# Four layers of conditioning and routed experts on 2048 tokens: routing matmuls reordered, expert places filled before the last shared down, a third job ahead of the experts, the last half as one program

## The chip, the cores and the metric

The kernel runs on one core of one Trainium2 chip. What is told is the device time of one execution in microseconds (us). The core has five engines that run their own instruction streams and wait for each other by semaphores: TensorE (PE, matmuls), VectorE (DVE), ScalarE (ACT), GpSimd (POOL) and SyncE (SP, which here only starts transfers); sixteen DMA engines move the data.

## The reference, cut to what matters

x is 2 x 1024 x 256 in float32. Four layers follow each other, each with a half that brings in the condition and a network half. The changed places lie in these halves:

```
swiglu(h) = (silu(h @ gate) * (h @ up)) @ down                             # 256 -> 512 -> 256
L0 ffn:  i = argmax(h @ gate_w)  (32 experts)
         x + swiglu_shared(h) + swiglu_i(h * sigmoid(max(h @ gate_w)))
L2 cond: s = sigmoid([h, t_emb] @ W_router.T); top 2 of 8 by s + bias, gates s / sum(s)
         (mean of 2 shared swiglu + sum of gates * gelu(h @ r_w1.T) @ r_w2.T) / 4
L2 ffn:  top 2 of 8 by softmax(h @ gate_W.T)
         x + 0.5 * shared swiglu (8 of width 128, mean) + 0.5 * gated swiglu of width 1024
L3 cond: as L2 cond, with one shared swiglu, divided by 3
L3 ffn:  top1 of 16 by softmax(h @ Wg); each expert takes its 160 tokens of highest probability
         y = h, and for taken tokens y = gelu(h @ W1 + b1) @ W2 + b2;   x + y
```

The output is x after the last layer, in float32.

## The kernel before, in words

A half is one `nc.Block`: a program for each engine, with a barrier at its end. In `half_l0`, `half_cond` (called for layers 2 and 3) and `half_ffn2` it runs in this order: the router's logits and their transposition (`pe_logits`, `pe_turn`); the first pieces of the shared unit; the places of the tokens among the experts' rows; the rest of the shared jobs; the routed experts; the jobs that are left, and the mixes.

The shared unit is class `Glu`. A job is 512 tokens through one unit. It has four up parts (`up_part`), each of which makes 128 columns of gate and up product in two banks of three pairs, and one `down`. Every matmul is split into three (`matmul_split`, L319 to L321) over high and low parts of both operands: `weights_high`, `features_high`, `hidden_high` are casts on ScalarE (L467, L459, L480), `weights_low`, `features_low`, `hidden_low` subtractions on VectorE (L491, L485, L504). Between up and down stand `silu` (L473, ScalarE) and `multiply` (L498, VectorE); a part of the same pair of banks waits for the multiply three parts earlier. `pe_jobs`, `act_jobs` and `dve_jobs` write out the order; `beside` is called behind each multiply, `between` behind each job. The number `split` says how many jobs precede the experts: four of eight in layer 2's cond half and in its network half, two of four in layer 3's cond half and in layer 0.

The places are class `Slots`: `scan` (L1252) on VectorE, `pe_places` (L1259 to L1265) on TensorE, `places` (L1272 to L1288) on VectorE, which gives each token its row, four times `mark` (L1297 to L1310) beside the parts, `pe_trace` (L1317, 32 or 16 groups of small matmuls) and `rows_of` (L1324 to L1331), from which gathers and scatters take their indices. In the cond halves the scatters L1458 write the rows sorted by expert to memory; they are paced by the multiplies, four for each step, and the experts load them from there (L586).

`LaneExperts` (layer 0) runs 24 rounds: in each, four lanes' weights are copied from the load's buffer `big` to their places in `space` (L1068), two parts on ScalarE and VectorE each, and then multiplied (L1106). `SplitGluExperts` (layer 2's network half) runs 39 tiles; its weights are cast to a high half by ScalarE (`own_highs`, L930) and a low one by VectorE (`own_lows`, L935). Both wait at their start for all shared downs, since the places lie in the shared unit's memory. In the trace, the last adds of the shared jobs are L1477 (layer 0), L1745 (layer 2's network half), L1608 and L1609 (cond halves); L1090, L943 and L661 turn the first rows of the experts. The mixes of the cond halves are L1717 and L1720, two adds for each of a chunk's four token tiles.

The last half is three programs. A route block (L3014) writes the rows to `by_token` and makes marks, trace and rows. `stage_sorted_biased` gathers row tiles (POOL L2785, two tiles for each semaphore), turns them (L2811), runs up (L2823), bias, gelu, turn (L2833) and down (L2844) for 31 tiles, adds the second bias (L2906) and scatters the results (L2795); the experts' weights come through a ring of four (`wring`, L2776, 1.4 MB each). Beside the tiles VectorE searches for each expert the bit pattern of the 160th highest probability, one bit in a tile (`try_bit`, L2914 to L2922), and TensorE sums the tally (L2851). `stage_kept_and_stored` ranks equal values, makes `keep` and `drop` (L2968 to L2983), adds both kinds of tokens (L2985, L2991; 16 each) and stores.

## Time and profile before

| what | us |
|---|---|
| median of three runs | 1734.08 |
| lowest and highest | 1731.73, 1737.95 |
| profiled execution | 1737.56 |
| its span in the trace | 1735.8 |

| stretch of the profiled execution (us from the start of the span) | what runs |
|---|---|
| 30.7 to 275 | layer 0, network half (lane rounds 93 to 262) |
| 409 to 689 | layer 2, cond half |
| 690 to 1276 | layer 2, network half (tiles 786 to 1190) |
| 1279.5 to 1511 | layer 3, cond half (experts 1365 to 1460) |
| 1511 to 1540 | route block of the last half |
| 1540 to 1711.7 | 31 tiles |
| 1711.8 to 1735.8 | kept and stored |

In the whole span TensorE is busy 1482 us (85%), VectorE 991 (57%), ScalarE 657 (38%), GpSimd 426 (25%), and the mean granted clock of TensorE is 0.915 of full speed. A share of the span says little here, since every stage has its own limit. The rows below are to be read by the idle time in brackets: it stands in front of the instruction, with what ended it.

### The profile page before, as it was taken

What the parts mean: (1) busy time and instruction counts of PE and PEld (TensorE: products, weight loads), DVE (VectorE), ACT (ScalarE), POOL (GpSimd) and SP (SyncE); (2) the same over time, 40 slices, a digit from 0 to 9 for tenths busy, and PEclk for the clock granted to TensorE, in tenths of its full rate; (3) what the DMA queues carried; (4) which work ended last, traced back from release to release, by engine and by line L of the source; (5) the groups of instructions that cost most, each with busy time, mean ns of one, the idle gap of its engine ahead of it and who ended that gap; (6) DMA issues with size and microseconds to landing.
All of it is one profiled execution on the core that took longest, in us unless ns stands there. A gap on an engine that the chain in (4) does not pass through costs nothing. (4 is left out here: it accounts for less than half of the span.)

```text
span 1735.8 us, 25954 instructions
## 1 busy us (share of the span) xinstructions
PE 1482.4 (85%) x8354; PEld 1126.5 (65%) x8354; DVE 991.0 (57%) x1782; ACT 657.1 (38%) x977; POOL 426.1 (25%) x366
## 2 busy tenths in 40 slices
PE   8787888765989997897999999999967799749992
PEld 5632334633877786786888888887856677526661
DVE  5566675435644364645877776774645334447675
ACT  3175775212233332224655555553322233201110
POOL 1512221000434400010343343331007243023420
PEclk9899999967899999898999999999987899859996
DMA  5268972352223240230222202204022233245823
GB/s 188 87 255 314 343 251 93 120 170 98 92 92 101 80 143 28 76 152 4 95 101 87 111 28 101 98 19 146 1 97 85 91 109 130 67 163 186 269 90 112
DMA packets 82918, 211.38 MB, mean 122 GB/s; under 512 B 10785, under 2 KB 57762, under 8 KB 74594
## 3 DMA queue, kind: packets, MB, share of 16 engines
q1 hardware_dynamic: 66944, 166.40, 26.9%
q0 software_dynamic: 15840, 43.27, 7.4%
q8 instruction: 76, 1.25, 0.3%
q14 instruction: 56, 0.46, 0.1%
q10 hardware_dynamic: 2, 0.00, 0.0%
HBM read 165.21 MB, written 44.43 MB: 121 GB/s over the span
## 5 line engine op out<-in xcount | busy, mean ns | idle before, releaser
L630 POOL DMA_INDIRECT results<-sb_big,sb_s_out_row x63 | 132.4, 2101 | 466.4 <-ACT sb_big L861 304.5
L935 DVE TENSOR_TENSOR sb_h_split<-sb_big,sb_h_split 128x2048 fp32r<-128x2048 f32 x78 | 178.5, 2289 | 87.9 <-ACT sb_h_split L930 87.9
L930 ACT CAST sb_h_split<-sb_big 128x2048 fp32r x78 | 146.7, 1903 | 42.0 <-issue 40.5
L826 PE MATMUL ps<-sb_big,sb_e_hT 128*128 x624 | 141.0, 379 | 1.1 <-DVE sb_e_hT L979 1.1
L319 PE MATMUL ps<-sb_h_split 128*128 128x512 f32 x312 | 133.5, 428 | 9.6 <-DVE sb_h_split L954 6.9
L1068 DVE COPY sb_g_space<-sb_big 128x1024 f32 x168 | 108.4, 699 | 49.8 <-issue 22.8
L1068 ACT COPY sb_g_space<-sb_big 128x1024 f32 x120 | 118.5, 1048 | 41.6 <-DMA sb_big<-in_l_routed 21.2
L826 PEld LDWEIGHTS ps<-sb_big,sb_e_hT 128*128 128x128 f32 x624 | 118.2, 190 | 18.5 <-issue 1.3
L319 PE MATMUL ps<-sb_g_split,sb_g_ws 128*128 128x512 f32 x256 | 108.5, 424 | 23.4 <-DVE sb_g_product L498 15.7
L1458 POOL DMA_INDIRECT sorted_in<-sb_big,sb_p_slots x64 | 70.4, 1099 | 220.3 <-DVE sb_p_slots L1284 177.3
L321 PE MATMUL ps<-sb_h_split 128*128 128x512 f32 x312 | 124.1, 398 | 0.0
L320 PE MATMUL ps<-sb_h_split 128*128 128x512 f32 x312 | 123.9, 397 | 0.0
L1106 PE MATMUL ps<-sb_g_space,sb_e_rT 128*32 128x512 f32 x768 | 95.7, 616 | 21.2 <-ACT sb_g_space L1068 9.6
L592 POOL DMA_INDIRECT results<-sb_big,sb_p_out_row x78 | 77.3, 992 | 147.3 <-DVE sb_big L741 146.7
L320 PE MATMUL ps<-sb_g_split,sb_g_ws 128*128 128x512 f32 x256 | 106.4, 416 | 0.0
L321 PE MATMUL ps<-sb_g_split,sb_g_ws 128*128 128x512 f32 x256 | 105.6, 412 | 0.0
L619 POOL DMA_INDIRECT sb_big<-by_token,sb_s_in_row x63 | 63.0, 1001 | 154.0 <-DVE sb_s_out_row L1331 135.4
L319 PE MATMUL ps<-sb_g_ws,sb_g_split 128*128 128x256 f32 x256 | 78.5, 307 | 25.2 <-DVE sb_g_split L504 14.5
L473 ACT ACTIVATE sb_g_sg<-ps 128x512 f32<-128x512 f32 x64 | 38.1, 597 | 148.4 <-PE ps L321 116.6
L673 PE MATMUL ps<-sb_big,sb_x_rT 128*128 x312 | 89.1, 409 | 4.1 <-ACT sb_x_rT L718 4.0
L498 DVE TENSOR_TENSOR sb_g_product<-sb_g_sg,ps 128x512 f32<-128x512 f32 x64 | 43.8, 685 | 68.0 <-ACT sb_g_sg L473 54.2
L693 PE MATMUL ps<-sb_big,sb_x_hT 128*128 x312 | 82.4, 388 | 0.0
(450 smaller groups left out, 3210.2 us busy)
## 6 DMA issues: line engine op xcount, KB each, us to landing
sb_big<-in_l_routed SPq DMA_DIRECT2D x32, 1024.0 KB
sb_big<-in_l2f_routed SPq DMA_DIRECT2D x8, 3072.0 KB, 10.5
sb_e_wring<-in_l_experts SPq DMA_DIRECT2D x16, 1408.0 KB
sb_big<-in_l_routed SPq DMA_DIRECT2D x32, 512.0 KB
sb_big<-results SPq DMA_DIRECT2D x32, 512.0 KB, 7.2
sb_big<-sorted_in SPq DMA_DIRECT2D x18, 512.0 KB
by_token<-sb_big SPq DMA_DIRECT2D x12, 512.0 KB, 3.2
sorted_in<-sb_l1p_zero SPq DMA_DIRECT2D x2, 2048.0 KB, 9.6
```

Source lines behind the costliest of these rows:

```text
L319: pe.matmul(to, w[0], x[0], start=start, stop=False)
L320: pe.matmul(to, w[0], x[1], start=False, stop=False)
L321: return pe.matmul(to, w[1], x[0], start=False, stop=stop)
L592: pool.indirect_dma_start(out=results, out_offset=bass.IndirectOffsetOnAxis(ap=places.out_row[:, j:j + 1], axis=0), in_=self.tile(j), in_o ...
L630: pool.indirect_dma_start(out=results, out_offset=bass.IndirectOffsetOnAxis(ap=places.out_row[:, j:j + 1], axis=0), in_=self.tile(j), in_o ...
L673: last = pe.matmul(psum[:, j % 2, 0:self.NF * P], self.rT[:, j % 2, k * P:(k + 1) * P], self.w[:, e, k * self.NF * P:(k + 1) * self.NF * P ...
L693: last = pe.matmul(psum[:, 2 + j % 2, 0:D], self.hT[:, j % 2, f * P:(f + 1) * P], self.w[:, e, lo:lo + D].rearrange("p s n -> p (s n)"), s ...
L826: last = pe.matmul(psum[:, 7, 0:D], self.hT[:, f // TPC, f % TPC * P:(f % TPC + 1) * P], self.weight(place, 2 * KD * self.F + f * D, D), s ...
L930: act.copy(self.own[part][:, 0, :], self.raw(e, part)).then_inc(self.own_high[part], 1)
L935: dve.tensor_tensor(self.own[part][:, 1, :], self.raw(e, part), self.own[part][:, 0, :], ALU.subtract).then_inc(self.own_low[part], 1)
L1068: last = copy(self.own[part][:, g, :], here.rearrange("p s n -> p (s n)"))
L1106: last = pe.matmul(psum[g * W:(g + 1) * W, 2 * part + u % 2, :], self.rT[:, r % 2, k, g * W:(g + 1) * W], self.own[part][:, g, lo:lo + FU] ...
```

## The change

1. In `half_l0`, `half_cond` and `half_ffn2` ScalarE makes four weight casts instead of two ahead of the quads; TensorE runs two up parts instead of three ahead of `pe_places`, and the third and fourth behind it; VectorE puts `multiply` ahead of `features_low`, and the last two weight subtractions go from ahead of the first multiply to behind the second and third. `pe_trace` waits for the marks by quarters.
2. `LaneExperts` and `SplitGluExperts` get `act_open` and `dve_open`, which fill the first expert's places during the last shared down, each part behind its own wait (`wait_space`); VectorE's part runs ahead of the last shared add (`closing`).
3. In layer 3's cond half `split` goes from two to three, the chunk order changes, and three mixes stand at the end instead of two.
4. The last half is one block, `half_ffn3`: the writes of the rows and the loads of the first experts stand on SyncE's queue at its start, each row tile has a semaphore, gathers follow the rows directly, the search starts at 2^-7 and has 26 steps instead of 30, the ranks, the choice and the adds of the dropped stand beside the last tiles, and loads and stores follow in the same block.

```diff
-TOP_BIT = 29
+TOP_BIT = 25
+FLOOR = 2.0 ** -7
...
             def dve_jobs(self, dve, n0, n1, between=None, beside=None, closing=None):
                 for m in range(self.NF * n0, self.NF * n1):
                     n, f = divmod(m, self.NF)
+                    self.multiply(dve, m)
                     if f == 0 and n + 1 < len(self.jobs) and n + 1 != self.resume:
                         self.features_low(dve, n + 1)
-                    self.multiply(dve, m)
...
                 self.hidden_low(dve, self.NF * n1 - 1)
+                if closing is not None:
+                    closing()
                 self.add(dve, n1 - 1)
...
+            def act_open(self, act, wait_space):        # SplitGluExperts
+                for part in range(2):
+                    wait_space(act, part)
+                    self.own_highs(act, 0, part)
...
+            def dve_open(self, dve):
+                for part in range(2):
+                    self.own_lows(dve, 0, part)
...
+            def dve_open(self, dve, wait_space):        # LaneExperts
                 experts = self.experts_of(dve, 0, (0, 1, 2))
-                self.fill_dve(dve, 0, 0, experts)
-                self.fill_dve(dve, 0, 1, experts)
+                for part in range(2):
+                    wait_space(dve, part)
+                    self.fill_dve(dve, 0, part, experts)
+                return experts
...
             def pe_trace(self, pe):
                 self.wait_known(pe)
-                pe.wait_ge(self.marked, 8)
                 for n in range(self.G):
+                    if n % (self.G // 4) == 0:
+                        pe.wait_ge(self.marked, 2 * (4 * n // self.G + 1))
...
+                def wait_space(eng, part):                                   # half_l0
+                    eng.wait_ge((glu.both, glu.downed)[part], (glu.NF * split, 2 * (split - 1))[part])
...
-                        for m in range(3):
+                        for m in range(2):
                             glu.up_part(pe, m)
                         places.pe_places(pe)
-                        glu.up_part(pe, 3)
+                        for m in range(2, 4):
+                            glu.up_part(pe, m)
...
-                        for q in range(2):
+                        for q in range(4):
                             glu.weights_high(act, 0, q)
                         route.act_quads(act)
-                        for q in range(2, 6):
+                        for q in range(4, 6):
                             glu.weights_high(act, 0, q)
...
-                        for q in range(4, 6):
-                            glu.weights_low(dve, 0, q)
                         def trace(m):
+                            if m in (1, 2):
+                                glu.weights_low(dve, 0, m + 3)
...
-                chunk_order = tuple(range(NCH)) if two else (2, 3, 0, 1)
+                early = () if two else tuple(range(split))
+                chunk_order = tuple(range(NCH)) if two else tuple(range(split, NCH)) + early
...
-                        if not two:
-                            mix(0, 2)
-                            mix(1, 3)
+                        for c in early:
+                            mix(c, N - split + c)
...
+                    def _(sp):                                               # half_ffn3
+                        for c in range(NCH):
+                            sp.dma_start(chunk_of(by_token, c), ctok[:, c * TPC:(c + 1) * TPC, :]).then_inc(written, 16)
                         for e in range(RING):
                             if e >= 2:
                                 sp.wait_ge(w_in[e % 2], 8 * (e - e % 2) + e % 2)
                             sp.dma_start(wring[:, e, :], a["l3_experts"][e]).then_inc(w_in[e % 2], 16)
+                        places.wait_known(sp)
...
+                        sp.wait_ge(stored, 16 * tiles)
+                        for c in range(NCH):
+                            load_results(sp, [y], c, got[c])
...
+                            if j == TOP_BIT + 1:
+                                rank_even()
+                            if j == TOP_BIT + 3:
+                                choose_kept()
                             if j >= 1:
                                 add_b2(j - 1)
+                            if j > TOP_BIT + 3:
+                                add_dropped((j - TOP_BIT - 4) * 6, (j - TOP_BIT - 3) * 6)
                         add_b2(tiles - 1)
+                        add_dropped((tiles - TOP_BIT - 4) * 6, NT)
...
-            half_cond(3, wr3c, bias3, ("g3",), [(0, c) for c in range(NCH)], 2, a["l3c_routed"], 1.0 / 3.0, None)
+            half_cond(3, wr3c, bias3, ("g3",), [(0, c) for c in range(NCH)], 3, a["l3c_routed"], 1.0 / 3.0, None)
+            half_ffn3()
```

VectorE in layer 3's cond half, from the last step of the places to the first mark, before (`sb_g_ws` is a weight part, `sb_g_split` the features, `sb_g_product` a multiply's output):

```order
2126 L1288 TENSOR_SCALAR sb_p_tile_expert<-ps 1x39
2127 L491 TENSOR_TENSOR sb_g_ws<-sb_wbuf,sb_g_ws 128x512 x2
2128 L485 TENSOR_TENSOR sb_g_split<-sb_big,sb_g_split 128x1024
2129 L498 TENSOR_TENSOR sb_g_product<-sb_g_sg,ps 128x512
2130 L1297 CAST sb_p_tall<-sb_p_slot 128x32
```

The same place now, up to the first of the two weight subtractions:

```order
2134 L1308 TENSOR_SCALAR sb_p_tile_expert<-ps 1x39
2135 L499 TENSOR_TENSOR sb_g_product<-sb_g_sg,ps 128x512
2136 L486 TENSOR_TENSOR sb_g_split<-sb_big,sb_g_split 128x1024
2137 L1317 CAST sb_p_tall<-sb_p_slot 128x32
2138 L1318 TENSOR_SCALAR sb_p_tall<-sb_p_tall 128x32
2139 L1319 CAST sb_p_high<-sb_p_tall 128x32
2140 L1320 SCALAR_TENSOR_TENSOR sb_p_slot<-sb_p_high,sb_p_slot 128x32
2141 L1325 TENSOR_TENSOR sb_big<-sb_lanes_iota,sb_p_high 128x312
2142 L1327 TENSOR_TENSOR sb_big<-sb_big,sb_ids 128x312
2143 L1330 TENSOR_TENSOR sb_big<-sb_lanes_iota,sb_p_slot 128x1024
2144 L499 TENSOR_TENSOR sb_g_product<-sb_g_sg,ps 128x512
2146 L492 TENSOR_TENSOR sb_g_ws<-sb_wbuf,sb_g_ws 128x512
```

The multiply moved ahead of three VectorE instructions, and the weight subtractions behind the first mark.

SyncE's transfers of the last half, before: the write of the rows in a block of its own, then the ring, and at the end loads and stores behind another block's end.

```order
262 L3015 UNCONDITIONAL_BRANCH
263 L3018 DMA by_token<-sb_big 128x4x256 x4
264 L3014 UNCONDITIONAL_BRANCH
265 L2771 UNCONDITIONAL_BRANCH
266 L2776 DMA sb_e_wring<-in_l_experts 128x2816 x4
...
303 L2770 UNCONDITIONAL_BRANCH
304 L2996 UNCONDITIONAL_BRANCH
305 L1464 DMA sb_big<-results 128x4x256 x4
306 L3002 DMA out_x<-sb_big 128x4x256 x4
```

The same transfers now:

```order
262 L2811 UNCONDITIONAL_BRANCH
263 L2814 DMA by_token<-sb_big 128x4x256 x4
264 L2818 DMA sb_e_wring<-in_l_experts 128x2816 x4
...
301 L1485 DMA sb_big<-results 128x4x256 x4
302 L2829 DMA out_x<-sb_big 128x4x256 x4
```

The ring's loads stand directly behind the rows' writes, and the ends of two blocks are gone from between.

VectorE at the end of the last tiles now (L2974 adds the second bias to a tile's rows, L2969 casts the last hidden tile, L3015 adds dropped tokens, L3052 kept ones):

```order
2802 L2974 TENSOR_TENSOR sb_big<-ps,sb_e_wring 128x256
2803 L3015 SCALAR_TENSOR_TENSOR sb_big<-sb_big,sb_e_drop 128x256 x6
2804 L2969 COPY sb_e_hT<-ps 128x512
2808 L2974 TENSOR_TENSOR sb_big<-ps,sb_e_wring 128x256
2809 L3015 SCALAR_TENSOR_TENSOR sb_big<-sb_big,sb_e_drop 128x256 x6
2813 L2974 TENSOR_TENSOR sb_big<-ps,sb_e_wring 128x256
2814 L3015 SCALAR_TENSOR_TENSOR sb_big<-sb_big,sb_e_drop 128x256 x4
2815 L3052 SCALAR_TENSOR_TENSOR sb_big<-sb_big,sb_e_keep 128x256 x16
```

Before, no add of dropped tokens stood among the tiles; all sixteen stood together in the block behind them.

## Rows read from the trace of the kernel before

**Rows 1.** Busy time by stretch: window, us, busy time (and count) by engine, clock, DMA.

```profile
93.00:262.00 169.00, 137.38 (x1414) 53.63 (x1418) 115.83 (x185) 123.86 (x167) 37.51 (x35) 0.96 0.81 299
785.00:1190.00 405.00, 394.18 (x1936) 334.99 (x1937) 288.90 (x280) 225.12 (x239) 135.05 (x69) 0.98 0.19 70
1556.00:1700.00 144.00, 133.05 (x568) 87.24 (x569) 99.85 (x296) 26.92 (x61) 46.96 (x48) 1.00 0.53 179
1713.00:1719.00 6.00, 2.67 (x6) 1.67 (x6) 3.77 (x11) 0.00 (x0) 0.00 (x0) 0.50 0.97 324
```

**Rows 2.** Order of time, VectorE, layer 3 cond: start, us, instruction, idle before.

```profile
1285.77 1.29 DVE L491 TENSOR_TENSOR sb_g_ws<-sb_wbuf,sb_g_ws 128x512 fp32r<-128x512 f32 x2 [2.74 <-ACT sb_g_ws L467]
...
1298.49 0.17 DVE L1272 TENSOR_SCALAR sb_p_count<-ps 128x8 int32<-128x8 f32 x1 [6.32 <-PE ps L1259]
...
1301.85 1.27 DVE L491 TENSOR_TENSOR sb_g_ws<-sb_wbuf,sb_g_ws 128x512 fp32r<-128x512 f32 x2
...
1304.18 0.67 DVE L498 TENSOR_TENSOR sb_g_product<-sb_g_sg,ps 128x512 f32<-128x512 f32 x1
```

**Rows 3.** Order of time, TensorE, the same stretch: first, 13th and 37th matmul, next part.

```profile
1287.12 0.80 PE L319 MATMUL ps<-sb_g_split,sb_g_ws 128*128 128x512 f32 x1 [1.18 <-DVE sb_g_ws L491]
...
1292.41 0.63 PE L319 MATMUL ps<-sb_g_split,sb_g_ws 128*128 128x512 f32 x1
...
1297.94 0.39 PE L321 MATMUL ps<-sb_g_split,sb_g_ws 128*128 128x512 f32 x1
...
1304.90 0.80 PE L319 MATMUL ps<-sb_g_split,sb_g_ws 128*128 128x512 f32 x1 [4.88 <-DVE sb_g_product L498]
```

**Rows 4.** Order of time, the same waits in layer 0 and in layer 2's halves.

```profile
52.21 0.80 PE L319 MATMUL ps<-sb_g_split,sb_g_ws 128*128 128x512 f32 x1 [5.92 <-DVE sb_g_product L498]
...
429.37 0.17 DVE L1272 TENSOR_SCALAR sb_p_count<-ps 128x8 int32<-128x8 f32 x1 [5.19 <-PE ps L1259]
...
704.90 0.17 DVE L1272 TENSOR_SCALAR sb_s_count<-ps 128x8 int32<-128x8 f32 x1 [3.23 <-PE ps L1259]
```

**Rows 5.** Order of time, TensorE, the first lane round of layer 0.

```profile
94.83 1.07 PE L1106 MATMUL ps<-sb_g_space,sb_e_rT 128*32 128x512 f32 x4 [2.96 <-DVE sb_g_space L1068]
```

**Rows 6.** Order of time, start of layer 2's 39 tiles: ScalarE, VectorE, TensorE.

```profile
785.40 3.70 ACT L930 CAST sb_h_split<-sb_big 128x2048 fp32r x2 [12.20 <-issue]
...
787.52 4.49 DVE L935 TENSOR_TENSOR sb_h_split<-sb_big,sb_h_split 128x2048 fp32r<-128x2048 f32 x2 [2.46 <-ACT sb_h_split L930]
...
792.41 0.80 PE L319 MATMUL ps<-sb_h_split 128*128 128x512 f32 x1 [6.85 <-DVE sb_h_split L954]
```

**Rows 7.** Order of time, layer 3 cond, between shared jobs and experts: TensorE, GpSimd.

```profile
1331.73 0.39 PE L319 MATMUL ps<-sb_g_ws,sb_g_split 128*128 128x256 f32 x1
...
1348.49 0.97 POOL L1458 DMA_INDIRECT sorted_in<-sb_big,sb_p_slots  x1 [0.30 <-issue]
...
1351.28 0.37 PE L319 MATMUL ps<-sb_g_ws,sb_g_split 128*128 128x256 f32 x1 [1.02 <-issue]
1352.68 0.37 PE L320 MATMUL ps<-sb_g_ws,sb_g_split 128*128 128x256 f32 x1 [1.03 <-issue]
...
1365.40 0.44 PE L661 MATMUL ps<-sb_ident,sb_big 128*128 128x128 f32 x2 [0.79 <-DVE sb_big L1608]
```

**Rows 8.** Order of time, end of layer 3's cond half: last down, last two mixes.

```profile
1492.17 0.58 PE L319 MATMUL ps<-sb_g_ws,sb_g_split 128*128 128x256 f32 x1 [4.26 <-DVE sb_g_split L504]
...
1501.27 6.79 DVE L1720 SCALAR_TENSOR_TENSOR sb_big<-sb_big,sb_t_gates 128x256 f32<-128x256 f32 x16
```

**Rows 9.** Order of time, start of the last half: trace, first gather, first turn.

```profile
1532.39 7.00 PE L1317 MATMUL ps<-sb_s_marks,sb_big 128*128 128x31 f32 x32 [7.44 <-DVE sb_big L1310]
...
1540.88 0.99 POOL L2785 DMA_INDIRECT sb_big<-by_token,sb_s_in_row  x1 [78.86 <-POOLq L3014]
...
1549.50 0.69 PE L2811 MATMUL ps<-sb_ident,sb_big 128*128 128x128 f32 x2 [10.10 <-DMA sb_big<-by_token,sb_s_in_row]
```

**Rows 10.** Order of time, VectorE, kept and stored: first step, adds of the kept.

```profile
1711.82 0.43 DVE L2968 TENSOR_TENSOR sb_k_over<-sb_val,sb_cut 128x256 f32<-128x256 f32 x1 [8.25 <-PEq L2770]
...
1724.53 6.42 DVE L2991 SCALAR_TENSOR_TENSOR sb_big<-sb_big,sb_k_keep 128x256 f32<-128x256 f32 x16
```

261 lines of the change are left out of this document (120 added, 141 removed).

## Prediction

> **What bounds the kernel now.** I read first the busy time by stretch [rows 1]. In the routed rounds of layer 2's network half TensorE is busy 394 of 405 us at a granted clock of 0.98, and in the last 31 tiles 133 of 144 us at 1.00: these stretches move only if TensorE gets less to do. In layer 0's lane rounds the DMA share is 0.81, so the loads share the bound with the copies on ScalarE and VectorE. What the change can shorten lies between such stretches. So I then read, stage by stage, the rows in order of time with what ended each idle time. The reader is to see in each of them one engine waiting for a chain of small steps on another.
>
> **Routing among the first pieces, four times.** In the layer 3 cond half TensorE runs three up parts from 1287.12 and only then the matmuls for the places; VectorE has been idle 6.32 us when it gets their result at 1298.49 [rows 2, 3]. Its chain for the places runs to 1301.85; then two weight casts and a feature cast (2.33 together) and the first multiply (0.67) follow, and TensorE, which needs that multiply to free a bank, has been idle 4.88 us at 1304.90 [rows 2, 3]. After the change TensorE runs two parts before the places. It starts them 1.18 us earlier, since VectorE no longer waits 2.74 us for ScalarE's third and fourth weight cast [rows 2]: these now stand ahead of the quads, where ScalarE was waiting for the logits. Twelve matmuls make a part; the first 13 come some 0.43 us apart (12 steps from 1287.12 to 1292.41), the others 0.23 (24 steps to 1297.94), so 13 x 0.43 + 11 x 0.23 = 8.1 us and the places come at 1294.0, VectorE's chain at 1294.4 instead of 1298.5. The multiply now stands ahead of the casts, and parts 2 and 3 fill TensorE's 4.88. From there VectorE's work beside the parts is the same in sum (the two weight casts only move behind multiplies 1 and 2) and fills its time, so what the chain gains is what is gained: **4.0** here (one part, 12 x 0.23 = 2.8, and 1.18), **3.8** in layer 2's cond half (idle 5.19) [rows 4]. In layer 2's network half the idle is 3.23, and only the part's 2.8 leaves: **2.7**. Layer 0 has less work for the marks (96 columns instead of 312), so TensorE is the bound after the places, and of its idle 5.92 all but the wait of about 1 us for the later quads is filled: **4.9** [rows 4]. The lows are bounded by 0 (the freed time is taken by the marks, which TensorE's trace then awaits in quarters), the highs by TensorE's own idle, 4.9 to 5.9.
>
> **First experts' places filled early.** In layer 0 TensorE waits 2.96 us for the first filled place at 94.83 [rows 5]; ScalarE's two and VectorE's two fills now run beside the last shared down. The 2.96 goes; as the copy frees the load's buffer some 18 us sooner, the next weights are requested earlier too, in a loop whose DMA share is 0.81 [rows 1]. I take **4.4**, between 2.4 (the idle, less a feature copy that stays) and 8. In layer 2's network half TensorE is idle 6.85 us until 792.41: ScalarE casts two halves only from 785.40, though it had been idle 12.20 us, and VectorE follows until 792.3 [rows 6]. After the change only the turn of the rows (785.12 to 785.56), its copy (0.36) and the low part (0.42) remain: the gate starts at 786.6, **5.8** earlier. The matmuls after this idle time come at 0.43 us instead of 0.23 for twelve in a row; with an idle time of 1 us the clock should stay: 12 x 0.2 = **2.3** more. Bounds: 3 (ScalarE's casts of 1.9 each late behind their wait) and 8.1. I take 8.1, since both engines were idle.
>
> **Third job before the experts.** From 1331.7 to 1365.4, the experts' first matmul, two downs of 48 matmuls x 0.12 = 5.9 us run on TensorE; the other 22 are waiting. From 1334.5 until 1352.7 it gets one matmul each 1.4 us, with no semaphore that ends its idle time, while GpSimd issues 32 scatters without a pause, the last at 1348.49 [rows 7]. The third job adds 48 x 0.23 = 11.1 and 5.9 = 17.0 us, and falls into these 22. Without the starving the experts start at 1331.6 - 4.0 + 11.1 + 3 x 5.9 + 2 = 1358.4, 7 us sooner; with all of it (its 18 us, of which half lies in matmuls that it only spreads) at 1367. I take 1363: 2.1 gained over all, the 4.0 above included. Behind the experts 17.0 leaves and one mix comes (8 x 0.42 = 3.4, [rows 8]); I allow 2.4 for the last down, which still waits for its hidden rows behind an add and a mix (4.26) and then runs at 0.21 a matmul: 11.2. Together **13.3**, from 9 to 18.
>
> The Trainium skill speaks to this starving: "Runtime: NRT & Kernel Launch", under Instruction fetch mechanics, says that an engine's sequencer fetches its next block of instructions by a DMA queue of its own while it runs the present one, and that this is mostly hidden. By that rule nothing would starve TensorE, the experts would start at 1358.4 and the total would be 4.6 us lower. The rows above do not agree: the gaps have no releaser and end with the burst of scatters; whether fetching is what they are, no row here shows.
>
> **The last half as one program.** *Start.* TensorE waits 7.44 us for all eight marks at 1532.39 and traces for 7.00 [rows 9]. The marks end 1.12 us apart, so the first quarter can start 3.4 earlier, and the trace then ends by its own pace: 3.4. Gathers start behind the block's end at 1540.88, and TensorE gets the first pair of row tiles only at 1549.50, after 10.10 us, because 5.8 MB of expert weights are loaded in the same time [rows 9]. Now three of four experts' weights are asked for at 1511 (2 MB of rows and 4.3 MB of weights are done by about 1530 at the 324 GB/s of the final load [rows 1]), each row tile has its own semaphore, and the pool needs no block end. Gather at 1536.9, landing some 3.6 us later: TensorE at 1540.5 instead of 1549.5, 9.0, and 0.3 of the short waits for weights in the first tiles: **9.3** with the 3.4 in it. Bounds 6 (gathers still wait on the fourth expert's 1.4 MB) and 11.
>
> *Tiles.* 31 tiles of 4.66 us stay, with TensorE busy 92% [rows 1]. Four search steps fewer take VectorE 4 x 2.3 us and TensorE nothing but four small matmuls (-0.5); the fp32 matmuls for the ranks cost about 1.4. So **-0.9**, and the 26 steps are worth nothing by themselves.
>
> *End.* The last row add ends at 1703.56, and VectorE idles 8.25 us until the next block [rows 10]; then the results are loaded, the choice of the kept takes VectorE until 1718.0, sixteen adds of the dropped 6.4, sixteen of the kept 6.4 (1724.53 to 1730.95), and the span ends 4.9 us after the last add [rows 10]. Now the choice lies in tile 28, but twelve of the dropped adds stand *ahead* of the last two casts and row adds: 6 x 0.40 = 2.4 before the last cast (which was not waiting) and 2.4 before the last row add; with the reads of the expert number (0.6 each) that add ends at 1706.8, 3.2 later than now. Scatter 0.3 + 0.97, landing 1.5: 1709.5; loads from 1709.6, the four chunks at about 1713.1 to 1717.6 (the 2 MB move within some 6 us now, 1713 to 1719 [rows 1]), last four adds 1.6, store 4.9: 1724.1. **11.7**, from 9 to 15.
>
> **Sum.** 4.0 is within cond 3's 13.3. Layer 0: 4.9 + 4.4 = 9.3; cond 2: 3.8; network half 2: 2.7 + 8.1 = 10.8; cond 3: 13.3; last half: 9.3 - 0.9 + 11.7 = 20.1. Together 57.3. The profiled execution took 1737.56 us (span 1735.8), so 1680.3 by it; the median of the three runs is 3.5 lower, 1734.08, and from that the change gives **1677**.
>
> **Rivals.**
> (A) *The gains are kept, as summed*: 1677, its own range 1668 to 1686. For it: each term is an idle time in a row, with its releaser, and the stretches between are bound by other things that the change leaves.
> (B) *Scatters starve TensorE again and the loads bound layer 0*: third job late (-6), fills in layer 0 worth 0 (-4.4), gathers at the start behind weights (-3), end at its low bound (-2.7): 16 less, 1693. For it: DMA share 0.81 and [rows 7]; against: in cond 2, where four jobs come first, downs run in 5.9 us beside scatters.
> (C) *More than summed*: no starving (+5), layer 0 at 8 (+3.6), the end at 15 (+3.3), the clock kept where idle times go (+3): 1662. By the page's rule on instruction fetching its first term comes by itself.
> (D) *VectorE is the bound in all four first stretches*, since its total of work is unchanged: the marks end as late as before, 4.0 + 3.8 + 2.7 + 4.9 lost, and the casts in layer 2 late (-5): 20 less, 1697. Against: 6.32, 5.19 and 3.23 us in which it did nothing just before the chain [rows 2, 4].
> (E) *Slower*: the routed rounds of layer 2 run at the low clock. They now begin without the long idle time, in another rhythm; at 0.43 instead of 0.23 us for each of twelve matmuls in two halves of 39 tiles the price is 39 x 2 x 12 x 0.2 = 187 us, and from 12 tiles on (58 us) it eats the sum. Against: 0.98 granted over 405 us [rows 1], and the low clock ended within 12 matmuls [rows 6]. If 16 tiles ran so, 1754.
>
> **How the numbers follow.** A 0.52, B 0.19, C 0.16, D 0.08, E 0.02, and 0.03 that something unseen takes back most of the sum (1728 to 1745). From 1660 to 1697 lies all of A, B, and most of C and D: about 0.83, so the range is 1659 to 1697. A measurement here tells 0.3% (5 us) from no change: faster in A to D and a little of the rest, 0.96; same 0.015; slower 0.025.
>
> **What would show it.** In the profile after: in the four first stretches no idle time of TensorE over 1 us ahead of the fourth part, and the places' first step 2.7 to 4.1 us sooner after the logits; the first gate of layer 2's tiles about 1 us after the turn; no row with an idle time of 1.0 us and no releaser in cond 3's downs, or else (B) again a matmul each 1.4 us; experts' first matmul there at a distance of 80 us from the first part (78.3 now); the first turn of rows 4 us after the first gather; the last row add some 3 us late against the last hidden cast, and 17 us from it to the end (32.2 now). Wrong would be the prediction if layer 0's rounds or layer 2's tiles changed their pace, for I took them as fixed.

## Result and the profile after

The changed kernel takes 1685.16 us (median of 4, 1683.05 to 1686.60) against 1734.23 for the kernel before in the same comparison: a ratio of 0.9713, with a 95% interval of 0.9694 to 0.9731. That is 49.1 us less. The forecast was 1677, or 57 less; its range of 1659 to 1697 holds the result. The profiled executions differ by 52.3 (span 1735.8 and 1683.5, mean granted clock 0.915 and 0.931).

I read the program by its stages. Each stage is taken from SyncE's first transfer in it to the first transfer of the next one, in both traces:

| stage | before | changed | forecast gain | measured gain |
|---|---|---|---|---|
| start | 30.8 | 31.5 | 0 | -0.7 |
| layer 0, network half | 262.1 | 251.7 | 9.3 | 10.4 |
| layer 1 (not touched) | 114.5 | 118.0 | 0 | -3.5 |
| layer 2, cond half | 282.5 | 276.1 | 3.8 | 6.4 |
| layer 2, network half | 589.6 | 580.0 | 10.8 | 9.6 |
| layer 3, cond half | 231.5 | 220.8 | 13.3 | 10.6 |
| last half | 224.8 | 205.4 | 20.1 | 19.4 |
| sum | 1735.8 | 1683.5 | 57.3 | 52.2 |

How far such a duration can be trusted is shown at the head of the first experiments: stages that nobody touched differ by 1 to 4 us from trace to trace.

Busy time by stretch, changed kernel (window, us, busy time and count of PE, PEld, DVE, ACT, POOL, granted clock, DMA share, GB/s), against [rows 1]. The three long loops have kept their pace; the prediction took them as fixed, and they are.

```profile
88.00:257.00 169.00, 139.94 (x1460) 54.95 (x1464) 117.64 (x188) 124.28 (x169) 41.13 (x36) 0.97 0.78 290
771.00:1166.00 395.00, 391.55 (x1929) 333.36 (x1930) 283.12 (x275) 221.10 (x237) 134.28 (x68) 0.99 0.20 71
1514.00:1658.00 144.00, 133.56 (x566) 88.52 (x566) 97.39 (x279) 26.72 (x61) 50.55 (x53) 0.99 0.50 170
```

The first pieces in layer 3's cond half, in order of time (start, us, instruction, idle before). Against [rows 2, 3]: VectorE waits 2.03 us for the places instead of 6.32, its multiply follows the places at once, and TensorE's 4.88 us ahead of a part are now 1.64. TensorE starts the first part without a wait.

```profile
1263.31 0.50 PE L320 MATMUL ps<-sb_g_split,sb_g_ws 128*128 128x512 f32 x1
...
1270.81 0.17 DVE L1292 TENSOR_SCALAR sb_p_count<-ps 128x8 int32<-128x8 f32 x1 [2.03 <-PE ps L1279]
...
1274.21 0.66 DVE L499 TENSOR_TENSOR sb_g_product<-sb_g_sg,ps 128x512 f32<-128x512 f32 x1
...
1279.68 0.47 PE L320 MATMUL ps<-sb_g_split,sb_g_ws 128*128 128x512 f32 x1 [1.64 <-DVE sb_g_product L499]
```

The start of layer 2's tiles, against [rows 6]. The casts run during the last down, and TensorE idles 1.05 us ahead of the first gate matmul (L320 on `sb_h_split`) instead of 6.85. One thing is late: VectorE's second low part ends at 768.96, after the last down (768.66), and the last shared add (L1773) stands behind it, so that the turn of the rows waits 1.55 us instead of 0.79.

```profile
762.34 1.91 ACT L933 CAST sb_h_split<-sb_big 128x2048 fp32r x1 [4.81 <-issue]
...
766.67 2.29 DVE L938 TENSOR_TENSOR sb_h_split<-sb_big,sb_h_split 128x2048 fp32r<-128x2048 f32 x1
768.88 0.68 DVE L1773 SCALAR_TENSOR_TENSOR sb_big<-ps,sb_big 128x512 f32<-128x512 f32 x1
...
771.70 0.50 PE L320 MATMUL ps<-sb_h_split 128*128 128x512 f32 x1 [1.05 <-DVE sb_h_split L957]
```

Between shared jobs and experts of layer 3's cond half, against [rows 7]. TensorE is again without work for no named reason while GpSimd scatters, now for 7 us instead of 18, and the experts start at 1344.31, 87.1 us into the stage (85.9 before).

```profile
1312.55 0.38 PE L320 MATMUL ps<-sb_g_ws,sb_g_split 128*128 128x256 f32 x1 [1.02 <-issue]
...
1313.24 0.97 POOL L1479 DMA_INDIRECT sorted_in<-sb_big,sb_p_slots  x1 [0.30 <-issue]
...
1314.67 0.28 PE L322 MATMUL ps<-sb_g_ws,sb_g_split 128*128 128x256 f32 x1 [1.63 <-issue]
...
1344.31 0.33 PE L664 MATMUL ps<-sb_ident,sb_big 128*128 128x128 f32 x1 [0.78 <-DVE sb_big L1636]
```

The last half, against [rows 9, 10]. TensorE's trace waits 4.08 us instead of 7.44 and the first turn 4.13 instead of 10.10. At the end the adds of dropped tokens stand between row adds, and the adds of the kept wait 5.21 us for the results.

```profile
1496.14 0.39 PE L1338 MATMUL ps<-sb_s_marks,sb_big 128*128 128x31 f32 x1 [4.08 <-DVE sb_big L1330]
...
1507.28 0.48 PE L2862 MATMUL ps<-sb_ident,sb_big 128*128 128x128 f32 x1 [4.13 <-DMA sb_big<-by_token,sb_s_in_row]
...
1661.15 2.46 DVE L3015 SCALAR_TENSOR_TENSOR sb_big<-sb_big,sb_e_drop 128x256 f32<-128x256 f32 x6
1664.44 0.42 DVE L2974 TENSOR_TENSOR sb_big<-ps,sb_e_wring 128x256 f32<-128x256 f32 x1 [0.83 <-DVE sb_big L3015]
...
1671.66 0.48 DVE L3052 SCALAR_TENSOR_TENSOR sb_big<-sb_big,sb_e_keep 128x256 f32<-128x256 f32 x1 [5.21 <-DMA sb_big<-results]
```

### The profile page after: what moved, and what is told of

The parts are those of the page before. It is cut to its first block and busy times, and to the rows that moved or that the text cites. A ratio compares the mean times of both kernels' runs of the same rounds, so it can differ in the third digit from the quotient of the medians.

```text
span 1683.5 us, 25908 instructions
## 1 busy us (share of the span) xinstructions
PE 1471.8 (87%) x8350; PEld 1117.3 (66%) x8350; DVE 984.0 (58%) x1754; ACT 656.8 (39%) x977; POOL 428.6 (25%) x366
## 5 line engine op out<-in xcount | busy, mean ns | idle before, releaser
L938 DVE TENSOR_TENSOR sb_h_split<-sb_big,sb_h_split 128x2048 fp32r<-128x2048 f32 x78 | 178.5, 2289 | 87.1 <-ACT sb_h_split L933 87.1
L320 PE MATMUL ps<-sb_h_split 128*128 128x512 f32 x312 | 133.1, 426 | 3.8 <-issue 2.8
L1479 POOL DMA_INDIRECT sorted_in<-sb_big,sb_p_slots x64 | 70.2, 1097 | 222.7 <-DVE sb_p_slots L1304 167.4
L320 PE MATMUL ps<-sb_g_split,sb_g_ws 128*128 128x512 f32 x256 | 107.0, 418 | 13.0 <-DVE sb_g_product L499 8.0
L1116 PE MATMUL ps<-sb_g_space,sb_e_rT 128*32 128x512 f32 x768 | 94.9, 611 | 19.4 <-issue 11.3
L321 PE MATMUL ps<-sb_g_split,sb_g_ws 128*128 128x512 f32 x256 | 104.0, 406 | 0.3 <-issue 0.3
L322 PE MATMUL ps<-sb_g_split,sb_g_ws 128*128 128x512 f32 x256 | 103.4, 404 | 0.0
L320 PE MATMUL ps<-sb_g_ws,sb_g_split 128*128 128x256 f32 x256 | 77.4, 303 | 22.9 <-DVE sb_g_split L505 21.3
## 6 DMA issues: line engine op xcount, KB each, us to landing
sb_big<-in_l2f_routed SPq DMA_DIRECT2D x8, 3072.0 KB, 10.6
```

The source lines that it names most:

```text
L320: pe.matmul(to, w[0], x[0], start=start, stop=False)
L321: pe.matmul(to, w[0], x[1], start=False, stop=False)
L322: return pe.matmul(to, w[1], x[0], start=False, stop=stop)
L938: dve.tensor_tensor(self.own[part][:, 1, :], self.raw(e, part), self.own[part][:, 0, :], ALU.subtract).then_inc(self.own_low[part], 1)
L1116: last = pe.matmul(psum[g * W:(g + 1) * W, 2 * part + u % 2, :], self.rT[:, r % 2, k, g * W:(g + 1) * W], self.own[part][:, g, lo:lo + FU] ...
```

## Experiments: each part taken back

Four kernels, measured together; the kernel before took 1735.15 beside them. Each is the changed kernel with one part undone. The difference of two medians is uncertain here by some 7 us, so the stages of the traces are read too. How much a stage differs with nothing changed in it can be seen in the changed kernel's trace and those of this group and the next one:

| stage | us in traces that leave it as in the changed kernel |
|---|---|
| layer 0, network half | 249.0 to 252.6 |
| layer 2, cond half | 276.1 to 278.6 |
| layer 2, network half | 580.0 to 581.6 |
| layer 3, cond half | 219.7 to 220.8 |
| last half | 204.4 to 208.1 |

The time from a stage's start to an event inside it can be much sharper: layer 0's first lane round starts 56.6 to 56.9 us into the stage in all six of its traces, and the spread arises in the 24 rounds behind it.

**u1_pieces**

```diff
-                        for m in range(2):
+                        for m in range(3):
                             glu.up_part(pe, m)
                         places.pe_places(pe)
-                        for m in range(2, 4):
-                            glu.up_part(pe, m)
+                        glu.up_part(pe, 3)
...
                         places.places(dve, link)
+                        for q in range(4, 6):
+                            glu.weights_low(dve, 0, q)
...
-                            if m in (1, 2):
-                                glu.weights_low(dve, 0, m + 3)
```

> The changed kernel with its first part taken back in all four stages: three up parts ahead of the places, two weight casts ahead of the quads, the multiply behind the feature subtraction, the last two weight subtractions ahead of the first multiply. The waits of the trace by quarters stay. Theory (the stage is bound by the chain through the places, and each term of the prediction is real): 4.9 + 3.8 + 2.7 + 4.0 = 15.4 us slower than the changed kernel, about 1700.5; by the changed kernel's trace (part 7 of layer 2's network half ends 3.0 sooner, of layer 3's cond half 4.2) the same within 1 us. Rival (the marks and VectorE's total set the time, so the order only shifts waiting): under 5 us, 1685 to 1690.

Measured: 1694.39, ratio 0.9750 (0.9707 to 0.9792), 9.2 over the changed kernel, between the theory's 15.4 and the rival's 5. By the stages of its trace layer 0 is 6.5 longer than in the changed kernel, layer 2's halves 3.2 and 3.0, layer 3's cond half only 0.5, 13.2 in all. Layer 0 is above the theory, and sharply so: the first lane round starts 62.9 us into the stage instead of 56.7. Layer 2's network half is as in the theory; its cond half, with 279.3 beside the 278.6 of an untouched one, is not clear of the spread. In layer 3's cond half TensorE's wait of 4.88 us is back and next to nothing is lost; the run u3_split2 bears on why.

**u2_fills**

```diff
-                        glu.dve_jobs(dve, 0, split, beside=trace, closing=lambda: experts.dve_open(dve))
+                        glu.dve_jobs(dve, 0, split, beside=trace)
                         dve.wait_ge(glu.downed, 2 * split)
+                        experts.dve_open(dve)
```

> The changed kernel with the first experts' places filled only after the last shared down, in layer 0 and in layer 2's network half. Prediction's terms: 4.4 + 8.1 = 12.5 us slower, 1697.7. By the changed kernel's trace the gate of layer 2's tiles starts 5.0 sooner after the last down and its first twelve matmuls still come 0.43 us apart, so without the clock's 2.3: about 5 there and 4.4 in layer 0, 9.5 slower, 1694.7. Rival (layer 0's rounds are bound by loads, which catch up): 5 slower, 1690.

Measured: 1702.72, ratio 0.9797 (0.9754 to 0.9839), 17.6 over the changed kernel; by its stages layer 0 is 6.1 longer and layer 2's network half 8.0, 14.1 in all. These durations overstate the part. In layer 0 the first lane round starts 3.8 us later than in the changed kernel; the rest arises in the rounds, which took 184.2 us here from the first to the last and between 179.7 and 183.6 in untouched traces, so whether the loads give time back is not shown. In layer 2's network half TensorE comes from the end of the last down to the gate in 8.07 us instead of 3.04, 5.0 more; 1.6 had been lost before that, beside the trace, where nothing was changed and where the untouched stage of u4_lasthalf lost the same, and 1.4 behind the last tile, as in other untouched stages too. So 3.8 and 5.0 are what this run shows for certain, and my correction to 9.5 was nearer than the prediction's 12.5.

```profile
92.82 1.93 PE L1116 MATMUL ps<-sb_g_space,sb_e_rT 128*32 128x512 f32 x8 [4.85 <-ACT sb_e_rT L1170]
...
779.87 0.44 PE L946 MATMUL ps<-sb_ident,sb_big 128*128 128x128 f32 x2 [0.78 <-DVE sb_big L1773]
787.15 0.80 PE L320 MATMUL ps<-sb_h_split 128*128 128x512 f32 x1 [6.85 <-DVE sb_h_split L957]
```

In layer 0 this part and the first together bring the first lane round 7.4 us forward (64.0 to 56.7 us into the stage); taken back alone they cost 6.3 and 3.8, so they overlap by 2.7.

**u3_split2**

```diff
-            half_cond(3, wr3c, bias3, ("g3",), [(0, c) for c in range(NCH)], 3, a["l3c_routed"], 1.0 / 3.0, None)
+            half_cond(3, wr3c, bias3, ("g3",), [(0, c) for c in range(NCH)], 2, a["l3c_routed"], 1.0 / 3.0, None)
```

> The changed kernel with two of four jobs ahead of the experts in layer 3's cond half, as before; all else stays. Prediction: 13.3 less the 4.0 of the first pieces = 9.3 slower, 1694.5. By the two traces: the experts there start 1.2 us later in their stage than before, of which the first pieces had given 4, and 11.9 are gained behind them: 6.7 slower, 1691.9. Theory of the starving (TensorE gets about one matmul per scatter once scatters have been issued for some 22 us without a pause, until 1 to 3 us after the last): with split 2 the burst is again 26 scatters long, and the starving lasts some 15 to 18 us instead of 7.

Measured: 1689.84, ratio 0.9739 (0.9700 to 0.9777), 4.7 over the changed kernel; the stage itself is 221.6, 0.8 longer. By the stage both expected costs, 9.3 and 6.7, are missed. TensorE's down(0) takes until 1323.1 instead of 1316.5, with GpSimd in a burst of 28 scatters from 1283.8 to 1320.7:

```profile
1319.76 0.97 POOL L1479 DMA_INDIRECT sorted_in<-sb_big,sb_p_slots  x1 [0.30 <-issue]
...
1320.61 0.37 PE L320 MATMUL ps<-sb_g_ws,sb_g_split 128*128 128x256 f32 x1 [2.22 <-issue]
...
1322.71 0.37 PE L322 MATMUL ps<-sb_g_ws,sb_g_split 128*128 128x256 f32 x1 [1.03 <-issue]
```

In u1, whose multiplies come at other times, the burst is 16 long and ends at 1327.2, and down(0), from 1324.8 on, idles only 0.3 us inside. So in this stage the two edits replace each other: each alone gives some 10, both together 10.6. That the rest is given back by what each does to the bursts is what these traces suggest.

**u4_lasthalf** (half_ffn3 replaced by the three programs of before, 30 steps)

```diff
-            half_ffn3()
+                stage_sorted_biased(route.onehots, route.top[:, 0, :], val, cut, places)
+                stage_kept_and_stored(val, cut)
```

> The changed kernel with its last half as three programs and 30 search steps, as before; the waits of the trace by quarters and all other parts stay. Prediction: 20.1 less the quarter waits' 3.4 = 16.7 slower, 1701.9. By the two traces the whole last half gave 19.4, so 16.0 slower. Rival (the single program gains only by the end; the start's 9.3 is mostly the quarter waits): 10 to 13 slower.

Measured: 1704.55, ratio 0.9824 (0.9784 to 0.9864), 19.4 over the changed kernel; the last half 221.0, 15.6 longer. The theory's 16.0 to 16.7 stands and the rival's 10 to 13 falls: the first turn comes 35.05 us into the stage instead of 29.20, so that 5.9 of the start's 9.3 are not the quarter waits'. The four undone parts sum to 50.9 by medians (9.2 + 17.6 + 4.7 + 19.4), for 49.1 gained; with 7 us of uncertainty in each, and parts that overlap, that agreement says little. By stages they sum to 43.7.

## Experiments: bursts, gathers, dropped adds

Again four measured together; the kernel before took 1735.64.

**s1_gaps** and **s2_early**

```diff
-                    pool.wait_ge(glu.multiplied, 3 + n * (glu.NF * split - 4) // (K * NT))
+                    pool.wait_ge(glu.multiplied, (4, 5, 6, 8, 8, 9, 10)[n // TPC - 1] if split == 3 else ...)   # s1
+                    pool.wait_ge(glu.multiplied, 1 + n // TPC if split == 3 else ...)                           # s2
```

> The changed kernel with the scatters of layer 3's cond half paced in shorter bursts: groups of four wait for the 4th, 5th, 6th, 8th, 8th, 9th and 10th multiply instead of the 4th to 10th. So the burst that was 20 long (1287.5 to 1314.2) becomes 12, a pause until the 8th multiply (1306.4), 8, a pause, 8. Theory S (what starves TensorE in its downs is a long unbroken burst: it sets in 22 to 26 us after the burst's start and ends 1 to 3 us after its last scatter): down(0) runs in 6 us instead of 12, parts 8 to 11 follow at once, the experts start about 7 us sooner and the kernel takes 5 to 7 less, 1679. Rival (it is the number of scatters in flight beside a down, or the stage is bound elsewhere): within 2 of 1685.

Measured: 1683.55, ratio 0.9706 (0.9681 to 0.9732): as a whole not to be told from the changed kernel, which is the rival's time. The stage is 215.6, 5.3 shorter and clear of its spread. Its trace has down(0) from 1303.25 to 1309.16, 5.9 us, beside scatters that began again at 1305.41 after a pause of 3.1. Theory S held for that burst; the second one became 16 long, and then VectorE took up the add of down(1) late and down(2) waited 4.1 us.

> The changed kernel with the scatters of layer 3's cond half paced by the 2nd to 8th multiply, so that they run nearly unbroken from 1274 (the places) to about 1306 and then four more. Theory S: TensorE would starve from 22 us into the burst, 1297, to about 1308; that stretch is its trace, part 7 and the start of down(0). If only downs starve (their matmuls come each 0.12 us, the others each 0.23 or slower), then hardly anything is lost, since the burst ends as down(0) begins: experts 5 us sooner, 1680. If any matmuls starve, part 7 is stretched by 5 to 8 us and the time stays at 1685 or above.

Measured: 1693.09, ratio 0.9757 (0.9721 to 0.9792), 7.9 over the changed kernel, the stage 224.2. All 32 scatters run unbroken from 1274.7 to 1319.9, and TensorE starves from 1310.5 on, not from 1297: the trace and part 7 went through undisturbed, down(0) did not, and after it part 8 was hit too:

```profile
1318.65 0.59 PE L320 MATMUL ps<-sb_g_split,sb_g_ws 128*128 128x512 f32 x1 [1.73 <-issue]
1319.35 0.59 PE L321 MATMUL ps<-sb_g_split,sb_g_ws 128*128 128x512 f32 x1
1320.75 0.59 PE L322 MATMUL ps<-sb_g_split,sb_g_ws 128*128 128x512 f32 x1 [0.81 <-issue]
```

So "22 us into a burst" is wrong as a rule. What the starved traces of the first two groups share is a burst of 20 or more, a down in it, and an end 1 to 3 us after the last scatter.

**g1_pause**

```diff
                 for j in range(min(self.DEPTH, self.tiles)):
+                    if pause is not None and j == 3:
+                        pause()                        # layer 0: pool.wait_ge(glu.downed, 2 * split)
                     self.gather(pool, j, places)
```

> The changed kernel with layer 0's first eight gathers split: three, then a wait for both shared downs, then five. In the changed kernel's trace VectorE takes up the second half of the first shared add only at 77.31, 4.3 us after TensorE's last matmul of down(0) and 1.4 after the last of the eight gathers; ScalarE's second fill waits until 77.41 for the same. Theory (unbroken GpSimd transfers hold these up, not the data): the add comes at 73.2, down(1) at 74.5 instead of 78.7, the first lane round 4 us sooner, and unless the loads catch up, layer 0 and the kernel 4 shorter (1681). Rival (the lane rounds are bound by the loads): the round starts sooner, the stage ends as now.

In the changed kernel, GpSimd's eight gathers end at 75.87, and VectorE's second half of the first shared add comes when TensorE's down has been over for 4 us; in g1_pause it comes at once. First the changed kernel's row, then that of g1_pause:

```profile
77.31 0.69 DVE L1498 TENSOR_TENSOR sb_big<-ps,sb_big 128x512 f32<-128x512 f32 x1 [6.32 <-remote]
```

```profile
75.12 0.69 DVE L1500 TENSOR_TENSOR sb_big<-ps,sb_big 128x512 f32<-128x512 f32 x1 [2.19 <-PE ps L322]
```

Measured: 1680.99, ratio 0.9684 (0.9662 to 0.9706), 4.2 under the changed kernel. The two ratios' intervals overlap. The first lane round starts at 84.22 instead of 88.14. The theory holds for the add and for the round. Layer 0 is 249.6, 2.1 shorter, but two untouched ones took 249.0 and 251.0, so whether anything of the 4 us reaches the end of the stage is not shown.

**d1_drops**

```diff
-                            if j > TOP_BIT + 3:
-                                add_dropped((j - TOP_BIT - 4) * 6, (j - TOP_BIT - 3) * 6)
                         add_b2(tiles - 1)
-                        add_dropped((tiles - TOP_BIT - 4) * 6, NT)
+                        add_dropped(0, NT)
```

> The changed kernel with all sixteen adds of dropped tokens behind the last row add, none among the last tiles. The prediction put 3.2 us of delay of the last row add on them; in the changed kernel's trace twelve adds stand ahead of it, and behind it VectorE idles 5.2 us and works 1.7 before the results land. Sixteen adds take 6.4 us, which fit. Expected: the last row add 3 us sooner, end 3 sooner, 1682. Rival (the last down is bound by TensorE's casts, not by the adds): under 1 us.

Measured: 1683.81, ratio 0.9705 (0.9680 to 0.9729), 1.3 under the changed kernel, which this measurement does not tell from nothing. In the trace the last row add ends 5.1 us after that of tile 28 (1656.21 to 1661.28) instead of 7.3 (1657.58 to 1664.86), and the sixteen adds end at 1667.6, 0.6 before the results are there:

```profile
1661.20 6.41 DVE L3015 SCALAR_TENSOR_TENSOR sb_big<-sb_big,sb_e_drop 128x256 f32<-128x256 f32 x16
1668.23 0.48 DVE L3050 SCALAR_TENSOR_TENSOR sb_big<-sb_big,sb_e_keep 128x256 f32<-128x256 f32 x1 [0.62 <-DMA sb_big<-results]
```

So the price of the twelve adds was 2.2 us for the last row add, where I had put 3.2.

## Experiments: joined, direct writes, 26 steps alone

The third four ran where the kernel before took 1722.36 (median of 15), 13 less than in the two groups above. The record puts the three groups on three different chips. Their times are compared with each other only.

**a2_again** (no edit)

> The changed kernel itself once more, as the measure for the three beside it: 1683 to 1687 by all theories, and for its stages 251 to 252 us in layer 0's network half, 221 in layer 3's cond half, 205 in the last half; layer 1, which the change does not touch, between 116 and 119 by what the clock grants there.

Measured: 1669.04, ratio 0.9701 (0.9670 to 0.9732), so the change is worth 53.3 here. Outside the expected times, and for a reason that the trace shows: with the same bursts, 20 scatters from 1277.3 to 1304.1, down(0) takes 5.9 us (1294.70 to 1300.60), no idle time is without a releaser, and the layer 3 cond stage takes 210.4 instead of 220.8. The experts start at 77.6 us of it instead of 87.1. Layer 0 takes 245.3, 6.3 less, of which 4.3 are there at the first lane round, since the shared add is taken up at once; layer 1 takes 114.3 and the last half 207.5, so of the stages' expected times none is met. Why these waits are absent here is not shown.

```profile
1325.45 0.33 PE L664 MATMUL ps<-sb_ident,sb_big 128*128 128x128 f32 x1 [0.79 <-DVE sb_big L1636]
```

**b1_steps26** (the kernel before, two constants)

```diff
-TOP_BIT = 29
+TOP_BIT = 25
+FLOOR = 2.0 ** -7
...
-                        link(dve.tensor_scalar(cut[:], iota_e[:, 0:E], 0.0, None, ALU.mult))
+                        link(dve.tensor_scalar(cut[:].bitcast(F32), iota_e[:, 0:E], 0.0, FLOOR, ALU.mult, ALU.add))
```

> The kernel before with 26 search steps instead of 30, starting at 2^-7, and nothing else changed. Prediction: the steps are hidden beside TensorE, worth nothing by themselves, at most 0.5 us from four small matmuls: ratio to before 1.000, tile stage as before within 1 us. Rival (VectorE's 2.3 us a step hold up the casts and row adds): 4 x 1 us or more faster.

Measured: 0.9996 (0.9979 to 1.0013). The four steps fewer are worth nothing by themselves. Its trace is also one of the old order in an unstarved execution: the two downs run in 5.9 and 6.0 us beside 28 scatters in a row, and then TensorE waits for the sorted rows:

```profile
1341.08 0.97 POOL L1459 DMA_INDIRECT sorted_in<-sb_big,sb_p_slots  x1 [0.31 <-issue]
...
1347.43 0.45 PE L662 MATMUL ps<-sb_ident,sb_big 128*128 128x128 f32 x1 [10.54 <-DMA sb_big<-sorted_in]
```

That is the cover of the third job: 10.5 us of waiting for rows here, 18 us of starving in [rows 7]. From this kernel to a2_again the stage goes from 222.7 to 210.4: the experts start 3.6 us later in it (74.0 and 77.6, with a third job ahead of them) and what follows is 15.9 shorter.

**n1_direct**

```diff
+                            for m in range(2 * NT):
+                                if m and m % TPC == 0:
+                                    sp.wait_ge(glu.multiplied, 3 + m * (glu.NF * split - 4) // (2 * NT))
+                                sp.dma_start(sorted_in[m * P:(m + 1) * P, :], xtok[:, m % NT, :]).then_inc(sent, 16)
```

> The changed kernel with the 32 scatters of layer 3's cond half replaced by 32 plain writes of the same 128 KB each on SyncE's queue, at the same places of the order, so the rows are not sorted by expert (that part of the computation is left out); bytes and destinations' tensor stay. Theory P (what starves TensorE and holds up the adds is GpSimd's issuing of indirect transfers, not the bytes): down(0) of that stage takes 5.9 us, no idle time without a releaser, the adds follow their downs at once. Rival (the bytes on the DMA engines): down(0) is stretched as before, by 3 us or more.

Inconclusive: 1676.27 in one run, the stage 211.6, down(0) 5.9 us, no idle time without a releaser. But a2_again beside it, with its indirect transfers, is as undisturbed, so the two theories are not told apart. Its whole time is no answer either: the last half, which was not touched, took 212.4 where a2_again's took 207.5.

**c1_joined** (g1_pause, d1_drops, and this pace)

```diff
+                    if split == 3:
+                        pool.wait_ge(glu.multiplied, (4, 5, 6, 8, 8, 9, 11)[n // TPC - 1])
+                        if n == 28:
+                            pool.wait_ge(glu.downed, 4)
```

> The changed kernel with three edits joined: the first gathers of layer 0 split in three and five; the scatters of layer 3's cond half in bursts of at most 12, the last four held until down(1) has ended; all adds of dropped tokens behind the last row add. If the three are independent, the stages give 2 + 6 + 1 us: about 1676 (1673 to 1679). Rival (the bursts only move to places where they hold up VectorE's adds instead): 1680 or more.

Measured: 1676.79, ratio 0.9728 (0.9703 to 0.9753), 7.8 over a2_again. The time lies in the edit meant as a cure: the last four scatters now wait for down(1), the load of the sorted rows is asked for at 1330.58, and TensorE idles for it, with the experts starting 81.6 us into the stage (77.6) and the first tiles at the low clock (0.67 granted over the first 21 us, 1.00 in a2_again); the stage takes 220.9 instead of 210.4.

```profile
1330.58 2.02 SPq L589 DMA_DIRECT2D sb_big<-sorted_in  x4
...
1334.51 0.45 PE L666 MATMUL ps<-sb_ident,sb_big 128*128 128x128 f32 x1 [3.99 <-DMA sb_big<-sorted_in]
```

Layer 0 is not shorter than in a2_again (247.0 and 245.3): where nothing holds the add up, the pause gives nothing. The last half is 5.2 shorter, of which d1_drops can explain some 2; the rest lies in the tiles' spread. The time falls in the expected 1673 to 1679, but that was worked out from the first two groups' level; against a2_again the joined edits are a loss, so this hit is luck.

## Why the prediction was right, and where it was off

The direction and the range hold, and so do the waits that were read as the cost: each of them is gone or shrunk in the rows. The sum was 5.1 too high against the profiled execution, and 8.2 against the medians. The other 3.1 are the base: I carried the gain of one profiled execution, 3.3 above its median, to the median.

Part of the agreement is luck. Layer 2's cond half gave 6.4 for 3.8 forecast, but its experts start only 3.6 sooner; the other 2.8 fall behind them, where nothing was changed: that stretch took 178.9 us in the trace of before, 176.1 now, and 175.2 in b1_steps26, which has the old order. Layer 0's 10.4 for 9.3 are 7.4 at the first lane round and 3.0 in rounds and tail that vary by more. Against these stand 3.5 lost in layer 1 and 0.7 at the start.

- **First pieces.** 4.0 + 3.8 + 2.7 + 4.9 forecast. Undoing shows 3.0 in layer 2's network half and 3.2 in its cond half, the latter not clear of the spread; layer 0 was worth 6.3. In layer 3 the places come 5.3 us sooner behind the router's turn (12.6 to 7.3; 4.1 worked out), but the gain is not additive to the third job: undone alone it costs 0.5.
- **Fills.** 12.5 forecast; 3.8 in layer 0 (4.4) and 5.0 for layer 2's idle time (5.8) are shown, the missing 0.8 being the last add behind VectorE's casts. The 2.3 for the clock is the step that is not borne out as worked out: in the changed kernel the idle times before the gate are down to 1.55 and 1.05 us, and the gate still ran its first nine matmuls at the low clock (granted 0.56). In u4_lasthalf, where this stage is the same and so are both idle times, it ran at the full clock (1.00):

```profile
774.12 0.50 PE L320 MATMUL ps<-sb_h_split 128*128 128x512 f32 x1 [1.04 <-DVE sb_h_split L957]
...
776.98 0.38 PE L946 MATMUL ps<-sb_ident,sb_big 128*128 128x128 f32 x2
```

From the gate to the next turn that is 2.86 us, against 4.43 in the changed kernel and 5.28 before. But u4_lasthalf had a longer stretch of low clock beside the trace and came to the gate 1.6 later, so both reach the next turn 98.9 to 99.0 us into the stage. With the fills undone it is 105.5: 6.6 for the 8.1 forecast. Two of the ten traces with fills are at 100.5, and against them it is 4.9.
- **Third job.** The step that failed is the start of the experts: 87.1 us into the stage, 1.2 later than before, where 2.1 sooner was taken (1363 against 1365.4 is 2.4; the sum lost 0.3 there). The bound named for full starving, 1367 in the time of before (1366.6 measured), is what came; behind the experts 11.8 were gained for 11.2 forecast. I had seen the starving in the rows and priced half of it.
- **The rule of the Trainium skill** ("Runtime: NRT & Kernel Launch", Instruction fetch mechanics). By that rule nothing would starve TensorE. In the first two groups it did, in the third it did not, with the same program; so neither the rule nor its contrary is shown, and the estimate that hung on it (experts 7 us sooner) is met only in the third group, where the experts start 77.6 us into the stage (78.9 by the forecast without starving).
- **Last half.** 9.3 at the start (38.5 to 29.2 us from the stage's first transfer to the first turn: 9.3 measured), -4.1 in tiles and dropped adds (-3.5 measured, in a stretch that varies by 4 us between untouched traces), 14.9 from the last row add to the end (32.2 to 18.6: 13.6 measured). The 26 steps are worth nothing, as said.
- **The signs named.** The first gate comes 1.49 us after the turn, and the experts of layer 3's cond half start 81.0 us after the first part, where 80 was named. Off are the wait ahead of the fifth part there (1.64, and none over 1 had been named up to the fourth), and the end, 18.6 us behind the last row add for 17.
- **Not seen in the rows.** In the kernel before, VectorE took up finished downs late: by 2.8 us in layer 0, 4.9 in layer 2's cond half and 17.3 in layer 3's. The prediction speaks of TensorE's starving only; the changed kernel has such waits too (4.2, 5.4 and 9.0).
- **Not in the sum.** Layer 1, untouched, took 3.5 more. Its instructions are the same; the granted clock over the changed kernel's stretches is 0.92 for 0.96 and 0.50 for 0.58. In the other traces this stage lies between 112.8 and 119.1. It is no effect of the change that could be shown, but it is as large as some terms of the sum.

## What to carry to other kernels

Where two edits feed the same wait (a faster chain, more work ahead of the same barrier), undo each alone before adding their gains: in layer 3's cond half each alone gave nearly all of it. Transfers that nobody needs yet can be put off, but only as long as the chain behind them keeps its slack: pauses between scatters cured one stall (s1_gaps), and cost 10 us when they made the experts wait 4 us for their rows (c1_joined). And a stage's duration is to be held against the same stage in traces that leave it alone before it is called a gain: here these differed by 1 to 4 us, where medians of four runs tell 7, and the time to an event close behind the edit told 0.3.

## What the runs showed of the hardware

With GpSimd issuing indirect transfers back to back (1.27 us each), TensorE's downs (a matmul each 0.12 us) came to one matmul per 1.4 us, and waits of VectorE on a finished half of a down ended 2 to 17 us late, most of them 1 to 3 us after the burst; ScalarE's second fill in layer 0 came at 77.41, 1.5 us after the last of eight gathers. The late waits are in every trace of the first two groups (in g1_pause not in layer 0, but in the cond halves), the starving in those whose burst of 20 or more meets a down; neither is in any of the third, with the same program. Shorter bursts removed one case each (down(0) in s1_gaps, layer 0's add in g1_pause); in s1_gaps late waits then came at down(1), 4.0 and 2.7 us. Whether it is GpSimd's issuing, the bytes, or the chip itself stays open: the record names three chips, two for groups that show it and another for the group that does not (and none for the first measurement), chip and hour cannot be told apart, and the run meant to tell (n1_direct) fell where there was nothing to tell. It goes with most of the difference between the old order's traces (16.9 us between the kernel before and b1_steps26): layer 3's cond half took 231.5 and 222.7, layer 0 262.1 and 256.5, with 5.0 of that ahead of the first lane round, and layer 2's cond half 282.5 and 277.6.

The granted clock is not fixed by the program: layer 2's network half, the same instructions with the same idle times, ran its first gate at the low clock in one trace and at the full clock in another, and layer 1 took 112.8 to 119.1 us.
